# A four-layer graph network on one core: 28 gathered tiles move from SyncE's single-row fetches to GpSimd

## The reference

```python
h = relu(layernorm(x))
x = x + mean_over_edges((h @ W)[src], dst) + b                                  # layer 0 
h = relu(layernorm(x))
lap = segment_sum(h[src] * edge_weight, dst)                                    # layer 1
x = x + normalize(leaky_relu((h + lap) @ W1 + (h * lap) @ W2 + b))
h = relu(layernorm(x))
m = (h @ Wn)[src] * edge_net(edge_attr)                                         # layer 2
x = x + mlp(segment_sum(m, dst))
h = relu(layernorm(x))
x = x + relu(layernorm(attention(h, src, dst, heads=4)))  + h                   # layer 3
```

## Time and profile before

| | us |
|---|---|
| median of 3 runs | 4186.21 |
| lowest and highest run | 4178.0, 4190.07 |
| span of the profiled execution, first to last instruction | 5348.7 |

### The profile page before, as it was taken

One profiled execution on the slowest core, in us unless ns is written; L12 is line 12 of the kernel. 1 busy time (PEld: TensorE's weight loads), 2 busy tenths in 40 slices (PEclk: granted clock), 3 DMA queues, 4 the chain that ended last, 5 costly groups with the idle time before them and its releaser, 6 DMA issues. The chain is left out here.

```text
span 5348.7 us, 68713 instructions
## 1 busy us (share of the span) xinstructions
PE 2667.0 (50%) x13316; PEld 2230.9 (42%) x13316; DVE 2614.4 (49%) x7231; ACT 1816.7 (34%) x4182; POOL 2997.4 (56%) x3172
## 2 busy tenths in 40 slices
PE   2555555544455555555333333333555555555557
PEld 1444444443344444445333333333444444444446
DVE  3333333333455555546333333333456667767678
ACT  2333333311233333312111111112345555656555
POOL 4556565555556555556355565555345555555553
PEclk7777777766777777767655565656667777767779
DMA  5333333322233333322222222223272111111110
GB/s 113 93 98 100 89 99 97 91 66 54 81 98 91 97 97 90 98 66 56 73 80 82 86 86 82 85 82 87 70 135 48 42 42 42 42 42 42 42 44 25
DMA packets 241787, 405.91 MB, mean 76 GB/s; under 512 B 67715, under 2 KB 140572, under 8 KB 241373
## 3 DMA queue, kind: packets, MB, share of 16 engines
q0 software_dynamic: 99456, 206.27, 15.7%
q10 hardware_dynamic: 74432, 122.18, 8.2%
q1 hardware_dynamic: 67484, 73.06, 4.8%
HBM read 331.63 MB, written 67.78 MB: 75 GB/s over the span
## 5 line engine op out<-in xcount | busy, mean ns | idle before, releaser
L683 POOL DMA_INDIRECT t_work<-d_T,t_tabG x3100 | 2926.8, 944 | 2183.9 <-SPq L781 1098.6
L1367 PE MATMUL ps<-t_work,t_acc 128*128 x2592 | 493.7, 355 | 647.6 <-SPq L762 459.1
L1367 PEld LDWEIGHTS ps<-t_work,t_acc 128*128 128x128 f32 x2592 | 440.9, 258 | 727.1 <-issue 726.7
L1428 DVE TENSOR_TENSOR t_acc<-t_acc,ps 128x128 f32 (+1 forms) x732 | 210.6, 288 | 914.8 <-remote 459.0
L1804 PE MATMUL ps<-t_work,t_hT 128*128 x1960 | 394.5, 363 | 339.0 <-ACT t_hT L1792 157.9
L1417 DVE TENSOR_TENSOR t_hT<-t_work,ps 128x512 f32<-128x512 f32 x244 | 167.2, 685 | 763.7 <-ACT ps L1504 615.0
L1804 PEld LDWEIGHTS ps<-t_work,t_hT 128*128 128x128 f32 x1960 | 337.5, 260 | 406.1 <-issue 406.1
L1367 PE MATMUL ps<-t_hT,t_acc 128*128 128x128 f32 x1296 | 275.2, 399 | 434.6 <-DVE t_acc L1428 313.0
L1504 ACT COPY ps<-t_acc 128x512 f32 x244 | 140.5, 588 | 1022.2 <-SPq L762 723.9
L596 ACT ACTIVATE t_acc<-ps,t_bcol 128x1024 f32<-128x1024 f32 x98 | 109.1, 1113 | 1079.6 <-DVE ps L609 587.4
L1367 PEld LDWEIGHTS ps<-t_hT,t_acc 128*128 128x128 f32 x1296 | 259.5, 306 | 452.6 <-DVE t_hT L1417 295.8
(11 more groups left out here) (189 smaller groups left out, 4469.0 us busy)
## 6 DMA issues: line engine op xcount, KB each, us to landing
d_edge_net<-t_acc ACTq DMA_DIRECT2D x98, 512.0 KB
t_acc<-d_edge_net SPq DMA_DIRECT2D x98, 512.0 KB
t_work<-d_T,t_tabG POOLq DMA_INDIRECT x3100
t_acc<-in_edge_attrT ACTq DMA_DIRECT2D x96, 512.0 KB
t_acc<-d_T SPq DMA_DIRECT2D x1792, 0.5 KB
t_acc<-d_T SPq DMA_DIRECT2D x896, 0.5 KB
t_work<-d_T SPq DMA_DIRECT2D x896, 0.5 KB
t_acc<-d_T ACTq DMA_DIRECT2D x12, 790.1 KB
```

The source lines that it names most:

```text
L683: pool.indirect_dma_start(out=work[:, at:at + width], out_offset=None, in_=table, in_offset=bass.IndirectOffsetOnAxis(ap=idx[:, g * QUAD + ...
L1367: last = pe.matmul(sums(layer, s, width), masks[s % MASKS][:, k, :], rows_k, start=(k == 0), stop=(k == QUAD - 1))
L1428: dve.tensor_tensor(out=o, in0=o, in1=sums(layer, s, width), op=ALU.add).then_inc(e_acc[layer], 1)
```

## The change

SyncE fetches no rows. GpSimd gathers all 782 tiles of each layer. The loop of SyncE is left with the register loads of `closed_at`, the waits and the two semaphore counts, and in layer 2 `load_net`.

```diff
-SIDE, SIDE_PER, SIDE_READ = 7, 5, 64
-SIDE_BEGIN = [-(-(P * j) // SIDE_PER) for j in range(SIDE + 1)]
-SIDE_AT = [SIDE_BEGIN[j + 1] + RING + 2 for j in range(SIDE)]
...
-            return min(QUAD, ET - QUAD * g) - (g in SIDE_AT)
+            return min(QUAD, ET - QUAD * g)
...
-        def fetch_rows(layer, table, n):
-
-            width = table.shape[1]
-            for c in range(SIDE_READS):
-                lo, hi = [min(max(SIDE_PER * m - SIDE_READ * c, 0), SIDE_READ) for m in (n, n + 1)]
-                if lo == hi:
-                    continue
-                if lo == 0:
-                    sp.wait_ge(s_src[c % 2], 16 * (SIDE_READS // 2 * layer + c // 2 + 1))
-                found = numbers(ENG.SP, side_sources(layer, c)[:, lo:hi], hi - lo, 0, N - 1)
-                for r, row in zip(range(c * SIDE_READ + lo, c * SIDE_READ + hi), found):
-                    j, p = divmod(r, P)
-                    sp.dma_start(side_rows(layer, j)[p:p + 1, 0:width], table[bass.ds(row, 1), :])\
-                        .then_inc(s_row[layer][j % 4], 16)
-                if hi == SIDE_READ and c + 2 < SIDE_READS:
-                    read_sources(layer, c + 2)
...
                 sp.wait_ge(GATHERED[n % RING], landed[n % RING] + gathered_by(n))
-                if n in SIDE_AT:
-                    sp.wait_ge(s_placed, 16 * (SIDE * layer + SIDE_AT.index(n) + 1))
                 sp.sem_inc(e_rdy[layer], QUAD)
...
-                fetch_rows(layer, table, n)
                 sp.wait_ge(used, ends[n % 4])
                 sp.sem_inc(e_free[layer], 1)
-                if n + RING in SIDE_AT:
-                    place_rows(layer, table, pitch, SIDE_AT.index(n + RING))
```

More of the change, by code:

```diff
@@ L40 @@
 assert STEPS % 2 == 0
-SIDE_READS = SIDE * P // SIDE_READ
-assert P % SIDE_READ == 0
-assert SIDE_AT[-1] < GROUPS
 assert GROUPS % 4 == 0 and 4 * HALFNET < STEPS
@@ L766, in relay_groups @@
                     load_net(n)
-            for c in range(2):
-                read_sources(layer, c)
             ahead = AHEAD if layer < 3 else AHEAD + 2
@@ L2007 @@
         "lastg": lastg.reshape(2, P).T, "lastrow": lastg[:GROUPS].reshape(1, GROUPS),
-        "sides": np.concatenate([src[QUAD * g + QUAD - 1] for g in SIDE_AT]).reshape(1, SIDE * P),
         "idx": src[:TILES].T, "dsts": dst[:TILES].T, "wgt": weight[:TILES].T,
```

## The result

The changed kernel takes 4218.59 us (4217.73 to 4221.76), the kernel before 4186.59 us in the same comparison (4178.0 to 4190.07). The ratio is 1.0079, with a 95% interval from 1.0064 to 1.0093: 32.0 us slower. Run once more beside the kernel before, in a later comparison, it was 1.0075 (1.0061 to 1.0088), 32.1 us.

A forecast was written before the change was run, and what follows sets the result against it. GpSimd was taken to bound the kernel, issuing gathers without a break inside each layer. The 28 added gathers gave +35 us (+26 to +54) and all other parts 0, so 4186.2 became 4221.2 us, range 4184 to 4236.

The forecast's parts named there:

- Part 1: GpSimd gets 28 more gathers, seven a layer, all on the path at 1.2486 us each: +34.96 us.
- Part 2: SyncE loses 3584 single-row DMAs, address arithmetic, register loads and 28 copies, hidden beside GpSimd in timed runs: 0.
- Parts 3 to 5: Last tile landing fourth in its group, DMA share of the 28 tiles, and start, pauses and tail: 0 each.
- Which waits of the profile exist in the timed runs: GpSimd's 1110 us of waiting for ring slots was taken as absent from timed runs, where it issues gathers without a break.
- the forecast of the new span: Span of the changed kernel's profile: 4274 us plus real waits at the starts of the layers, 4260 to 4330.
- the cleaned profile: First profile of the kernel before, 5348.7 us, without GpSimd's 1110 us of waits: 4239 us, 53 us over the median.
- A sign that did not come: VectorE's and TensorE's waits ending at SyncE's line 762 shrink, and the gathers become what they end at; no size given.
- The late SyncE: Rival: SyncE is late in timed runs too, so removing its rows gains; 4108 us at the extreme, 4164 with half; chance 0.11.
- Layer 3 is VectorE's: Rival: small waits make VectorE bind layer 3, hiding seven gathers; 21 count, 26.2 us, 4212.4 us; chance 0.11.
- The readers' pace: Rival: the readers set the pace everywhere and GpSimd's time is slack: 0, 4186 us; chance 0.08.
- A longer gather: Rival: gathers beside the others get longer, priced at the trace's longest: 54.2 us, 4240.4 us; chance 0.04.
- the locked port: Skill's rule of 3.1 us for a GpSimd DMA beside a locking VectorE copy: 87 us, 4273 us; not counted.

The follow-up runs named there:

- the undisturbed profile: The kernel before, unchanged, profiled once more: 4185.37 us, with a span of 4184.1 us.
- the kernel without the rows: Changed kernel with the 28 tiles gathered by nobody: SyncE fetches no rows, GpSimd leaves out the last tile of seven groups a layer; 4183.55 us, ratio 0.9995.

## Why the prediction was right, and where it was not

The forecast was 4221.2 us and the median is 4218.6, inside the range of 4184 to 4236 and on the side that had 0.81.

**Part 1, 28 gathers at the distance between starts, +34.96 us.** Right. Taking exactly these gathers away gave back 35.0 us, and 36.8 us more lie between the first and the last gather. The duration alone, 26.4 us, would have been too little. The rule of the Trainium skill (Perfetto Trace Analysis, "GPSIMD Engine Instruction") on distances between starts holds here: 0.947 us is shown, 1.252 us is what a gather takes.

**Part 2, SyncE's work at nothing.** Right within a few us. Two kernels that differ from the old and from the new one in SyncE's rows alone put it at 2.7 and 2.6 us, and both are inside the scatter; it would be the difference between 35 and the measured 32. "A pass of 3.4 us beside 4.99" was too short by 0.4: the undisturbed profile has 3.78 us of work in a pass, since the sum took one load and five rows and little besides. The room that is left, 1.2 us, was still enough.

**Parts 3 to 5, placing, DMA share, start, pauses and tail at nothing.** Start and tail moved by 3.1 and 1.2 us between two profiles, which single executions can't tell from nothing. No run takes placing or the DMA share by itself; with part 2 they are together within the 3 us between 35 and 32.

**Which waits of the profile exist in the timed runs.** The conclusion was right, that GpSimd issues without a break, and it carried the forecast. One reason under it was not: "Such a hold-up can't be in the timed runs at this size" was read as a property of a profiled execution, and I expected a span 50 to 100 us over the median. Two later profiles with all of SyncE's rows, and the changed kernel's own, agree with the timed time within 1.5 us. The step that failed is the forecast of the new span, 4260 to 4330 us: it is 4216.6. The 53 us by which the cleaned profile still lay over the median were in the pauses and the tail, that the disturbed execution had stretched as well: from 31.7 + 64.3 + 70.5 us to 21.7, 47.4 and 47.1, and the tail from 134.7 to 123.6, together 61 us.

A sign that did not come: VectorE's and TensorE's waits that end at SyncE's line 762 should have shrunk, with the gathers named in their place. TensorE's largest such wait went from 671 to 635 us, ScalarE's grew from 724 to 790, and both still name SyncE, since the readers wait for its count and not for the gather. VectorE's went from 92 to 41. In the undisturbed profile of the kernel before the three are 660, 772 and 34 us, so the change moved none of them by more than some 25.

**The late SyncE (0.11).** Out, by the kernel without the rows. As a threshold it is real: at seven rows a pass SyncE does bind, three tiles away from where the kernel stands. My price for its pass, a load of 1.1 us whatever its size and 0.41 to 0.45 for each row, left out that the load grows with its numbers; at five rows that makes no difference.

**Layer 3 is VectorE's (0.11).** The mechanism is real and close, but not reached: GpSimd still sets the pace there, by 43 us in 984. All 28 gathers count, the seven of layer 3 too (8.9 us).

**The readers' pace (0.08).** Out: 28 gathers less were 35 us less.

**A longer gather (0.04), and the locked port.** The longest gather after the change is 1.757 us, the median 0.947 against 0.944. (VectorE's busy time beside the gathers is 408 to 910 us a layer in the earlier trace rows, not 421 to 910.) The Trainium skill's 3.1 us for a GpSimd DMA beside a locking VectorE copy (SBUF — State Buffer, "A bandwidth-pool intuition that's wrong (but worth ruling out)") is shown by no run here.

## What to carry to other kernels

Before a profile is read for its waits, hold its span against the timed runs: here the largest wait of the first profile, 987 us, was not in the kernel at all, and a fix of it would have been worth nothing. Where one queue issues without a break, each of its instructions is worth its distance from start to start: 28 of them at 1.25 us are 35 us, and the median moved by 32. An engine with slack can take some of them until its own pass meets that pace. That point is to be computed with every instruction that an item costs, here some 0.2 us of register load beside 0.41 us of issue, since beyond it the loss is far larger than the gain was: one tile more than before won 5.7 us, three more cost 109.

## What had not been expected of the hardware

- One profiled execution of five thousand microseconds had SyncE's instructions held up again and again, register arithmetic included (37 ns, up to 1416), and gave 5349 us instead of 4184. Six other profiles with 3584 to 7168 rows show none (arithmetic takes at most 51 ns in the one with 7168).
- A load of numbers into SyncE's registers costs about 0.2 us for each number in layers 0 to 2, from 0.83 us for three to 2.23 for ten, but 1.44 us for ten in layer 3; the four numbers of the closing table took 0.49 us beside the single rows and 0.30 us without them.
- With seven rows a pass, SyncE still waits for 211 us in the run, and the kernel is already 109 us slower than with five. A sum of waits over the run hides where they lie: nearly all of these are where a layer begins or ends, while inside layer 0 a pass takes 5.19 us, over the 4.99 of GpSimd.
- The fastest kernel of the study with the reference's result is the one with eight tiles and six rows a pass: 0.9988 of the kernel before (0.9979 to 0.9997) and 38 us under the changed kernel on the same chip.
